# One normed-expert stage: the seventh expert's rows summed in PSUM, the last expert's squares added in two parts

## The reference, cut to what matters

```
h = relu(xt @ W1[e] + b1[e])                    # 128 -> 512, each of 8 experts
h = layernorm(h) * g1[e] + be1[e]
y = relu(h @ W2[e] + b2[e])                     # 512 -> 128
y = layernorm(y) * g2[e] + be2[e]
gate = top-2 softmax weights of the router, spread over the 8 experts
out = sum over e of gate[:, e] * y[e]
x = x + tanh(g_ffn[1]) * out
```

## Time and profile before

| | us |
|---|---|
| median of 3 runs | 1508.92 (1506.22 to 1510.54) |
| the profiled execution's own time | 1507.92 |
| its span | 1506.1 |
| PE busy | 1332.3 (88%) |
| PE weight loads busy | 881.5 (59%) |
| DVE busy | 1095.9 (73%) |
| ACT busy | 749.6 (50%) |
| POOL busy | 340.0 (23%) |

### The profile page before, as it was taken

One profiled execution on the slowest core, in us unless ns is written; L12 is line 12 of the kernel. 1 busy time (PEld: TensorE's weight loads), 2 busy tenths in 40 slices (PEclk: granted clock), 3 DMA queues, 4 the chain that ended last, 5 costly groups with the idle time before them and its releaser, 6 DMA issues.

```text
span 1506.1 us, 28464 instructions
## 1 busy us (share of the span) xinstructions
PE 1332.3 (88%) x10892; PEld 881.5 (59%) x10892; DVE 1095.9 (73%) x3289; ACT 749.6 (50%) x1422; POOL 340.0 (23%) x282
## 2 busy tenths in 40 slices
PE   4789988897998998889898999989899899888987
PEld 3456745565665664456565575546566567445755
DVE  3556977877667696687775787778676669778774
ACT  0155635664344653575434553566543555357642
POOL 1021210540131220162003032044112112115300
PEclk7799999999999999999999998999999999999999
DMA  9000000000000000000000000000000000000000
GB/s 355 23 1 1 1 1 1 2 2 18 1 8 2 1 1 2 1 1 2 18 1 8 2 1 1 2 0 2 17 2 8 2 1 1 2 1 1 2 1 8
DMA packets 15095, 18.94 MB, mean 13 GB/s; under 512 B 2777, under 2 KB 13673, under 8 KB 14445
## 3 DMA queue, kind: packets, MB, share of 16 engines
q1 hardware_dynamic: 14960, 17.13, 3.4%
HBM read 16.08 MB, written 1.05 MB: 11 GB/s over the span
## 4 chain that ended last, share of the span: by engine, by line
PE 54%; DVE 28%; issue 6%; ACT 6%; POOL 2%; DVEq 0%; POOLq 0%; ACTq 0%
PE bank L1054 8%; PE bank L1065 6%; PE bank L1493 4%; PE bank L1498 4%; PE bank L1287 4%; DVE work L651 3%; DVE small L650 3%; DVE small L657 3%; PE bank L862 2%; PE bank L1486 2%; PE bank L1529 2%; PE bank L502 2%; PE bank L1916 2%; PE bank L1901 2%; PE bank L1572 2%
## 5 line engine op out<-in xcount | busy, mean ns | idle before, releaser
L267 POOL TENSOR_TENSOR root<-variance,minus_half 128x2 f32<-128x2 f32 (+1 forms) x72 | 55.2, 767 | 619.1 <-DVE variance L284 392.5
L1109 ACT ACTIVATE work<-bank,w_f 128x512 f32<-128x512 f32 x128 | 87.9, 687 | 92.2 <-PE bank L1054 91.9
L1065 PEld LDWEIGHTS bank<-w_f1d,work 128*128 128x128 f32 x1024 | 119.1, 192 | 13.4 <-issue 13.4
L1667 ACT ACTIVATE work<-work,small 128x128 f32<-128x128 f32 x256 | 78.3, 388 | 84.8 <-DVE small L1794 84.8
L1054 PE MATMUL bank<-xnT,w_f 128*128 128x512 f32 x256 | 120.2, 616 | 0.0
L1065 PE MATMUL bank<-w_f1d,work 128*128 128x129 f32 x1024 | 119.9, 275 | 0.0
L1725 POOL TENSOR_TENSOR small<-small 128x16 f32<-128x16 f32 x32 | 92.9, 2902 | 106.3 <-DVE small L1753 104.6
L1752 DVE TENSOR_REDUCE small<-work 128x16 f32<-128x1024 f32 x48 | 58.4, 1217 | 42.6 <-ACT work L1631 40.9
L650 DVE TENSOR_REDUCE small<-bank 128x8 f32<-128x512 f32 x96 | 65.7, 684 | 31.2 <-PE bank L510 30.9
L1493 PE MATMUL bank<-w_x,cxT 128*128 128x512 f32 x128 | 63.9, 622 | 21.9 <-DVE work L1766 17.1
L1498 PEld LDWEIGHTS bank<-consts,work 128*128 128x128 f32 x576 | 64.2, 140 | 29.2 <-issue 16.8
(11 more groups left out here) (290 smaller groups left out, 3145.6 us busy)
## 6 DMA issues: line engine op xcount, KB each, us to landing
w_f<-in_f_dram SPq DMA_DIRECT2D x1, 2616.0 KB
w_f<-in_f_dram SPq DMA_DIRECT2D x1, 2180.0 KB, 25.7
w_x<-in_x_dram SPq DMA_DIRECT2D x1, 2115.0 KB
w_l<-in_l_dram SPq DMA_DIRECT2D x1, 2088.5 KB, 21.1
w_f1d<-in_f1d_dram SPq DMA_DIRECT2D x4, 512.0 KB
work<-in_x_dram SPq DMA_DIRECT2D x4, 256.0 KB, 3.6
work<-in_ctx_dram SPq DMA_DIRECT2D x4, 256.0 KB, 3.9
out_dram<-x SPq DMA_DIRECT2D x4, 256.0 KB, 2.3
```

The costliest lines, as they stand in the source:

```text
L1065: pe.matmul(z_of(e, t)[:, 0:129], hT[e % 2][:, c, t * P:(t + 1) * P], w_f1d[:, c, e, :], start=(c == 0), stop=(c == 3))
L1109: act.activation(hT[e % 2][:, c, :], banks[n % 3][:, :], ACT.Relu, bias=k_f1["b1"][:, n:n + 1]).then_inc(hT_ready, 1)
L1667: ins = act.activation(s_sb[b % 2][:, c * P:(c + 1) * P], s_sb[b % 2][:, c * P:(c + 1) * P], ACT.Exp, bias=negmax[b % 2][:, c:c + 1])
```

## The change

The last expert's squares are folded by DVE once instead of twice, and PE sums both halves with eight one-column matmuls instead of four. The seventh expert's rows (index 6, `EXPERTS - 2`) are no longer added to x by DVE. ACT multiplies them in place by their weights, after its sixth piece of masked keys, and PE adds them with an identity matmul for each tile into the same bank as the means. The two filling matmuls between the coefficients' transposes and the means are gone, and those behind the means are four instead of two. DVE waits for one add_expert fewer.

```diff
                     def sum_squares(e):
                         pe.wait_ge(squares_summed, due(squares_summed, e + 1))
+                        parts = 2 if e == EXPERTS - 1 else 1
                         for t in range(TILES):
-                            m = pe.matmul(z_of(e, t)[:, 129:130], sq[e % 2][:, 0, t * P:(t + 1) * P], ones[:, 0:1],
-                                          start=True, stop=True)
+                            for c in range(parts):
+                                m = pe.matmul(z_of(e, t)[:, 129:130], sq[e % 2][:, c, t * P:(t + 1) * P], ones[:, 0:1],
+                                              start=(c == 0), stop=(c == parts - 1))
                         m.then_inc(down_done, 1)
...
                     m.then_inc(combT_done, 1)
-                    keep_clock(pe, banks[1], 2)
+                    pe.wait_ge(y_weighted, due(y_weighted, 1))
                     pe.wait_ge(combT_ready, due(combT_ready, 1))
                     for t in range(TILES):
+                        pe.matmul(banks[3][:, t * D:(t + 1) * D], ident, y[(EXPERTS - 2) % 2][:, t, :],
+                                  start=True, stop=False)
                         m = pe.matmul(banks[3][:, t * D:(t + 1) * D], combT[:, t * P:(t + 1) * P], w_f1b[:, :],
-                                      start=True, stop=True)
+                                      start=False, stop=True)
                     m.then_inc(means_done, 1)
-                    keep_clock(pe, banks[1], 2)
+                    keep_clock(pe, banks[1], 4)
...
                         if h == 5:
+                            act.wait_ge(coef_ready, due(coef_ready, 1))
+                            e = EXPERTS - 2
+                            for t in range(TILES):
+                                weighted = act.activation(y[e % 2][:, t, :], y[e % 2][:, t, :], ACT.Identity,
+                                                          scale=w2[:, t, e:e + 1])
+                            weighted.then_inc(y_weighted, 1)
                             act.wait_ge(combT_done, due(combT_done, 1))
...
                     def add_squares(e):
                         dve.wait_ge(squared, due(squared, e + 1))
-                        link(dve.tensor_tensor(sq[e % 2][:, 0:2, :], sq[e % 2][:, 0:2, :], sq[e % 2][:, 2:4, :], ALU.add))
+                        halves = dve.tensor_tensor(sq[e % 2][:, 0:2, :], sq[e % 2][:, 0:2, :], sq[e % 2][:, 2:4, :], ALU.add)
+                        if e == EXPERTS - 1:
+                            halves.then_inc(squares_summed, 1)
+                            return
+                        link(halves)
...
-                        if e >= 1:
+                        if 1 <= e < LAST:
                             add_expert(e - 1)
...
-                    dve.wait_ge(x_added, due(x_added, LAST))
+                    dve.wait_ge(x_added, due(x_added, LAST - 1))
```

More of the change, by code:

```diff
@@ L1029, in body @@
                      first_variance, first_root, y_raw, second_variance, second_root, x_added, coef_ready,
-                     combT_done, combT_ready, means_done, means_added):
+                     combT_done, combT_ready, means_done, means_added, y_weighted):
                 def z_of(e, t):
@@ L1251, in ffn1 @@
             stage("routed:1 half:1 sig:1 up:32 hT:32 sq_sum:8 squared:8 down:8 var1:8 root1:8 y_raw:8 var2:8 "
-                  "root2:8 x_added:7 coef:1 combTd:1 combTr:1 means_done:1 means_added:1", body)
+                  "root2:8 x_added:6 coef:1 combTd:1 combTr:1 means_done:1 means_added:1 y_weighted:1", body)
             return ends[0]
```

## The result

The changed kernel takes 1526.27 us (median of 4 runs, 1524.41 to 1526.49), beside 1507.57 us for the kernel before in the same runs (1504.83 to 1510.54). The ratio is 1.0127, 95% interval 1.011 to 1.0143: 18.7 us slower. Slower was forecast, but 1514.2 with 1523 as the upper end was too low. Three executions at a clearly lower granted clock (0.741 to 0.839), two of the kernel before and one of an experiment, took 1609.82 to 1751.87 us and are left out of every time and ratio here.

The account below looks back on a forecast made before the run. DVE's chain was taken to bound the stage's end, and PE everything after the turn. 4 x 0.0 (order at full clock) + 3 x 3.4 (falls) - 3.9 = +6.3 us on 1507.92: 1514.2 us, range 1505 to 1523.

Parts of the forecast that it names:

- DVE: End of stage: POOL's root holds DVE, which scales at about 199.12 instead of 200.01, reaching the means' addition 0.9 us earlier.
- PE's sums and ACT: Ahead of the means: ACT's keys start 0.36 us later, four weightings take 1.27 us, PE may start the means at 201.4.
- PE's means: At the means: sixteen records take 2.2 us (bounds 1.8 and 2.5) instead of 1.08 for eight, ending at about 203.6.
- The filling: Behind the means: twelve records instead of 8 hold PE 5.2 us, to 208.7, so the first turn gains nothing.
- The clock: Right ahead of the means: the granted clock falls in three blocks of four, costing 3.4 us each (low time 6.8).
- rival (d): At the stage's end all four blocks fall, for 10.24 us each: +16.5 us, 1524; chance 0.12.
- Rival (a): At the stage's end falls come but are short, 3.41 us: 4 blocks with 1.2 us each, about 1509; chance 0.20.
- The 3.9 us of the falls before: Clock loss around the turns in blocks 2 and 3 of the kernel before, expected to be gone: -3.9 us.
- my guess that the long fall belonged to this very work: Block 3 of the kernel before: the one 10.24 us fall was put down to small 16-row matmuls and fillings.

Follow-up runs that it names:

- 128 rows for 16: Changed kernel with the means' 16-row matmuls replaced by 128-row identity matmuls on a tile of ones, the means' part left out; 1506.27 us, ratio 1.0004.
- rows only: Changed kernel with the diff's squares' part taken back; 1526.11 us, ratio 1.0151 to the kernel before.
- wide identity: Changed kernel with one 512-column identity matmul in place of four of 128 columns, ahead of the four 16-row matmuls; 1516.48 us, ratio 1.0083.
- two behind: Changed kernel with two filling matmuls behind the means instead of four, none between transposes and means; 1515.67 us, ratio 1.0071.
- squares only: Kernel before with only the squares' part of the change; 1506.39 us, ratio 1.0008.

## Why the prediction was wrong, step by step

**DVE: right.** Counted from the last fold's start, the scaling of the last expert was to come 199.12 - 192.15 = 6.97 us later, held by POOL; it came 200.56 - 193.65 = 6.91 later, released by POOL's L1149.

**PE's sums and ACT: right.** ACT's keys 3.51 us after the fold forecast, 3.36 measured; the four weightings 1.27 and 1.26; the means could start 9.25 us after the fold by the forecast and did at 8.92.

**PE's means: wrong, outside the bounds.** This is the first term that failed. I priced sixteen records by eight that all had 16 rows, 2.2 us, and gave 2.5 as the upper end. They take 3.3 at full clock and 5.76 at half. The row priced one kind of weights at a time. The change mixed two kinds.

**The filling: right in mechanism.** PE, not the rows, was to set the turn, and does, by 2.7 us in block 1 (rows done at 212.27 + 0.60 = 212.87, turn at 215.55). At full clock the twelve records' 5.2 us could be held against 5.16 in the kernel with 128 rows for 16 (1283.18 to 1288.34).

**The clock: right in kind, mis-sized twice.** This is the second term that failed, and by far the larger one. A fall ahead of the means was the forecast's mechanism. I had it in three blocks of four, at 3.4 us. It came in four, and the turn was later by 5.4, 5.1, 5.0 and 4.1 us than 16.5, sum 19.5 with the pairs' cost in it, where the forecast had 10.2. The low time was 10.2 us in three blocks and 6.8 in one, where I took 6.8; rival (d), rated 0.12, was the nearest, at 1524. (Rival (a) had 1.2 us a fall, for which no row is given; half of 3.41 is 1.7, which would put it at 1511.) The 3.9 us of the falls before were indeed saved: 19.5 - 3.9 = 15.6, the 15.5 of the stage's end. How the 19.5 divide is an estimate: at full clock the turn would stand 8.92 (means start) + 3.3 (pairs) + 5.16 (fillings) = 17.4 us after the fold, 0.9 later than before, so the pairs make some 3.5 us in four blocks, where the sum had 0.0, and the low clock some 16, where it had 3 x 3.4 = 10.2.

Why four: the emptied place. I called the new stretch emptier than any before, and by the rows it isn't: PE is busy 0.60 us in 3.37, against 0.44 in 3.45 ahead of the turns of before, where one in three was followed by a fall. But where the filling stands decides. In the five kernels that have none between transposes and means (changed, rows only, wide identity, two behind, 128 rows for 16) the clock falls ahead of the first turn in 19 of 20 stage ends; in the nine that have two there, in 10 of 36. With the wide identity and the squares' part in both, it is four blocks against none. The one-column sums that were added are not needed for it: rows only, without them, falls in all four. Each count comes from one execution, but the others agree: the mean granted clock was 0.963 to 0.966 in all four executions of the changed kernel, 0.958 to 0.966 in those of rows only, and 0.970 to 0.985 in those of the kernel before.

Why long: the 16-row matmuls, as far as shown. Of the 16 falls in the four kernels with 16-row matmuls right behind the emptied place, 13 last 10.2 us and three 6.8. With 128 rows in their place the same idle time is followed by 6.8 us of low clock at most, in one kernel and three falls. That the longer group is what stretches the fall doesn't fit: wide identity's group takes 3.75 us at half clock, the one with 128 rows 3.46 (200.73 to 204.19), and yet the first has three long falls and the second none. So my guess that the long fall belonged to this very work is borne out for the emptied place, and I then averaged it away with falls on other work. Why block 3 of the kernel before, with its filling between, had a long one is open: the ten other falls ahead of a turn with filling between lasted 6.8 us at most.

The rule of the Trainium skill (TensorE: Matmul & The Clock Gate, section "What's actually happening"), that activity releases the throttle, is not borne out here as I read it: in block 1 PE was busy 9.73 of 10.20 us and the clock stayed at 0.50 all that time. By that rule, as the prediction read it, the falls would have cost 1.7 us each at most, an estimate from the 3.41 us falls before.

**Not in the sum.** The clock fell ten times instead of seven outside the stage, 2.9 us. These falls come and go between profiles of the other kernels also (the kernel with squares only has fewer than before). From profile to profile, what isn't between the last fold and the second turn takes 1415.6 to 1422.0 us in the fourteen kernels, with four to ten falls; the kernel before is at 1419.2 and the changed one at 1422.0, the highest. No run ties these 2.9 us to the change, and this part stays open.

## What to carry to other kernels

What matmuls that fill PE's idle time are worth depends on where they stand. Here, moved out of the last gap ahead of urgent work, they left that work at half clock in nearly every block, and stacked ahead of a turn they delayed it. When matmuls with few rows and with many go into one sum, do all of one kind first (here one wide identity matmul, then the small ones). And a price for a group of matmuls taken from rows of one shape isn't a bound for a mixture.

## What the runs showed of the hardware that I had not expected

Two-record matmuls of 128 columns in turn with 128-row and 16-row weights start 0.41 us apart at full clock and 0.72 at half. All with 128 rows they start 0.22 and 0.43 apart, and in a group of 16-row matmuls alone eight records take 1.08 us, that is 0.27 for two (at half clock 2.01 us, 0.50 for two, in block 3 of the kernel before). After the same idle time of 2.1 us ahead of the means, the low clock lasted 10.2 us in nine of the twelve stage ends of the changed kernel, the one with the wide identity matmul and the one with two filling matmuls behind, and never over 6.8 in the one with 128 rows throughout.
